# The second attention's first two adjacency tiles are prepared one phase earlier

## The reference, cut to what matters

```
qkv    = layernorm(x) @ Wqkv + bqkv
scores = q k^T / 8 + graph_bias * adj
scores = where(adj == 0, -1e9, scores)
x      = x + softmax(scores) v @ Wout + bout
```

## Time and profile before

| | |
|---|---|
| time, median of 3 runs | 2719.99 us (2716.86 to 2720.1) |
| the profiled execution: time | 2717.6 us |
| its span, and what lies around it | 2715.9 us, 1.7 us |
| p1: first DMA issued | 1144.85 us |
| a1: first DMA issued | 1224.11 us |
| first score added on DVE | 1239.55 us |

### The profile page before, as it was taken

One profiled execution on the slowest core, in us unless ns is written; L12 is line 12 of the kernel. 1 busy time (PEld: TensorE's weight loads), 2 busy tenths in 40 slices (PEclk: granted clock), 3 DMA queues, 4 the chain that ended last, 5 costly groups with the idle time before them and its releaser, 6 DMA issues. The chain is left out here.

```text
span 2715.9 us, 59651 instructions
## 1 busy us (share of the span) xinstructions
PE 2481.9 (91%) x20186; PEld 2029.7 (75%) x20187; DVE 2011.5 (74%) x4258; ACT 1614.1 (59%) x3050; POOL 1426.9 (53%) x1747
## 2 busy tenths in 40 slices
PE   6799999999975999097999999999689999999999
PEld 5377777777764998075777777777578888888888
DVE  5899989899945443787777777777667777777776
ACT  1577777777730332244666666666467777777775
POOL 6366666666451554432111122111388888888886
PEclk9799999999976999598999999999899999999999
DMA  2011111111054222301111111110000000000001
GB/s 99 21 43 49 56 43 43 43 63 43 22 197 148 70 72 62 126 16 35 55 41 41 41 41 41 45 58 21 7 1 0 0 0 0 0 0 0 0 0 41
DMA packets 43885, 114.26 MB, mean 42 GB/s; under 512 B 5621, under 2 KB 29918, under 8 KB 37982
## 3 DMA queue, kind: packets, MB, share of 16 engines
q1 hardware_dynamic: 38174, 97.16, 10.2%
q0 software_dynamic: 5568, 15.21, 1.8%
HBM read 99.21 MB, written 13.15 MB: 41 GB/s over the span
## 5 line engine op out<-in xcount | busy, mean ns | idle before, releaser
L2145 PE MATMUL f_pm<-f_wl,f_yt 128*128 128x256 f32 x2640 | 625.6, 380 | 0.0
L2145 PEld LDWEIGHTS f_pm<-f_wl,f_yt 128*128 128x128 f32 x2640 | 477.2, 191 | 51.6
L1089 POOL TENSOR_TENSOR ADJ<-ADJ,a_off 128x2708 f32<-128x2708 f32 x22 | 131.2, 5962 | 543.1 <-DVE ADJ L1168 543.1
L118 POOL TENSOR_SCALAR f_yy<-f_th,f_rs 128x255 f32<-128x255 f32 x660 | 367.5, 573 | 21.8 <-POOL f_rs L113 21.8
L526 ACT COPY a_wt<-a_tp 128x512 f32<-128x512 f32 x528 | 256.9, 566 | 155.3 <-PE a_tp L732 155.3
L1995 DVE SCALAR_TENSOR_TENSOR f_gg<-f_th,f_pm 128x512 f32<-128x512 f32 x319 | 219.0, 687 | 171.4 <-ACT f_th L2089 170.3
L549 POOL TENSOR_SCALAR a_off<-ADJ 128x677 bf16<-128x677 f32 x84 | 278.3, 3334 | 78.3 <-DMA ADJ<-in_adj 63.7
L626 DVE SCALAR_TENSOR_TENSOR a_lg<-a_f1s,F2S,a_fo 128x1024 f32<-128x1024 f32 (+1 forms) x264 | 294.5, 1152 | 30.8 <-issue 17.1
L1148 DVE CUSTOM_DVE_ANT_0 a_sc<-a_qk,ADJ 128x1024 f32<-128x1024 f32 (+1 forms) x264 | 288.3, 1093 | 30.4 <-PE a_qk L1246 30.4
L2089 ACT ACTIVATE f_th<-f_pm 128x512 f32<-128x512 f32 x319 | 190.5, 597 | 199.7 <-PE f_pm L2145 199.7
L1112 ACT ACTIVATE a_sc<-a_sc,a_mx 128x1024 f32<-128x1024 f32 (+1 forms) x264 | 277.7, 1052 | 45.3 <-DVE a_mx L1153 45.3
(11 more groups left out here) (295 smaller groups left out, 4572.0 us busy)
## 6 DMA issues: line engine op xcount, KB each, us to landing
ADJ<-in_adj SPq DMA_DIRECT2D x44, 1354.0 KB, 5.8
W<-in_L_ffn_w SPq DMA_DIRECT2D x32, 512.0 KB, 9.8
m_got<-YD SPq DMA_DIRECT2D x6, 768.0 KB, 10.4
out<-X SPq DMA_DIRECT2D x21, 128.0 KB
X<-in_x SPq DMA_DIRECT2D x3, 768.0 KB, 9.9
XD<-XF SPq DMA_DIRECT2D x3, 768.0 KB
m_b<-in_L_ffn_b SPq DMA_DIRECT2D x1, 2048.0 KB, 8.4
m_rows<-XD,SLOT POOLq DMA_INDIRECT x58, 2.8
```

The costliest lines, as they stand in the source:

```text
L118: return eng.tensor_scalar(out, x, rs[:, 0, bass.ds(t, 1)], rs[:, 1, bass.ds(t, 1)], ALU.mult, ALU.add)
L2145: mm = pe.matmul(out, yt[:, g, r, k, :], wl[:, k, :], start=(k == 0), stop=(k == KD - 1))
```

## The change

The three steps for the first two adjacency tiles move from the start of `a1` into `p1`; `off`, `gb` and their semaphores are allocated for both phases, and `gb` is loaded in `p1` ahead of the adjacency tiles. In `p1` DVE does `off` and the scaling of tile 0 after the statistics and before `results(0)`, and those of tile 1 after `results(4)`. POOL does the sum of tile 0 after it has normalised tile t = 5, and that of tile 1 after t = 15. In `a1` DVE goes straight to its first score. PE no longer waits ahead of its first score; it waits for `wout` alone, after the nine chunks, before its loop. POOL waits for `bout` alone.

```diff
+ADDED = (5, 15)
 def layer1_prepare(nc, io, keep, layer1):
...
             sp.dma_start(bv[:, :], bcast_rows(io["L1_gnn_bqkv"][2 * D:3 * D], P)).then_inc(b_in, 16)
-            first_adj(sp, io, layer1["ADJ1"], layer1["adj_in"])
+            sp.dma_start(gb[:, :], io["L1_gnn_graph_bias"].rearrange("a b c -> (a b) c").to_broadcast([P, 1])
+                         ).then_inc(gb_in, 16)
+            first_adj(sp, io, adj, adj_in)
...
                 standard_rows(pool, xn[:, t % 4:t % 4 + 1, :], X[:, t:t + 1, :], rs, t).then_inc(xn_done[b], 1)
+                if t in ADDED:
+                    k = ADDED.index(t)
+                    pool.wait_ge(scaled_adj[k], 1)
+                    pool.wait_ge(off_done[k], 1)
+                    pool.tensor_tensor(adj[:, k, :], adj[:, k, :], off[:, :], ALU.add).then_inc(bias_done[k], 1)
...
         def _(dve):
+            def first_tile(k):
+                dve.wait_ge(adj_in[k], 16)
+                if k:
+                    dve.wait_ge(bias_done[0], 1)
+                else:
+                    dve.wait_ge(gb_in, 16)
+                dve.tensor_scalar(off[:, :], adj[:, k, :], 0.0, MASKED, ALU.is_equal, ALU.mult).then_inc(off_done[k], 1)
+                dve.wait_ge(off_done[k], 1)
+                dve.tensor_scalar(adj[:, k, :], adj[:, k, :], gb[:, :], None, ALU.mult).then_inc(scaled_adj[k], 1)
             dve.memset(V[:, :, :, HD:VW], 1.0)
             slot_moments(dve, X, st, mom, stats, folded, moments)
             dve.wait_ge(b_in, 32)
+            first_tile(0)
...
             for i in range(NPAIR):
                 results(i)
+                if 2 * i + 1 == ADDED[0] + 4:
+                    first_tile(1)
...
 def layer1_attention(nc, io, keep, layer1):
...
-            sp.dma_start(gb[:, :], io["L1_gnn_graph_bias"].rearrange("a b c -> (a b) c").to_broadcast([P, 1])
-                         ).then_inc(gb_in, 16)
-            sp.dma_start(wout[:, :, :], io["L1_gnn_Wout"].rearrange("(k p) o -> p k o", p=P)).then_inc(w_in, 16)
-            sp.dma_start(bout[:, :], bcast_rows(io["L1_gnn_bout"], P)).then_inc(w_in, 16)
+            sp.dma_start(wout[:, :, :], io["L1_gnn_Wout"].rearrange("(k p) o -> p k o", p=P)).then_inc(wout_in, 16)
+            sp.dma_start(bout[:, :], bcast_rows(io["L1_gnn_bout"], P)).then_inc(bout_in, 16)
...
-            for b in range(2):
-                bias(0, b)
-            pool.wait_ge(w_in, 32)
+            pool.wait_ge(bout_in, 16)
...
-            dve.wait_ge(gb_in, 16)
-            for b in range(2):
-                off_tile(0, b)
-                scale_tile(0, b)
...
-            pe.wait_ge(w_in, 32)
             for h in range(3):
                 for c in range(NC):
                     scores((0, 0, h), c)
+            pe.wait_ge(wout_in, 16)
```

More of the change, by code:

```diff
@@ L797, in _ @@
             turn_back(last_unit(H - 2))
+ADDED = (5, 15)
 def layer1_prepare(nc, io, keep, layer1):
     X, V, ident, neg_half = (keep[n] for n in ("X", "V", "ident", "neg_half"))
-    QT, KH, KL = (layer1[n] for n in ("QT", "KH", "KL"))
+    QT, KH, KL, off, gb, adj, adj_in, off_done, scaled_adj, bias_done = (
+        layer1[n] for n in ("QT", "KH", "KL", "OFF1", "GB1", "ADJ1", "adj_in", "off_done", "scaled_adj", "bias_done"))
     W2 = 2 * P
@@ L822, in layer1_prepare @@
         pv = ph.ps("pv", [P, 2, 512])
-        (w_in, b_in, scaled, kept0, kept, stats, moments, inv, pchain, folded, masked,
+        (w_in, b_in, gb_in, scaled, kept0, kept, stats, moments, inv, pchain, folded, masked,
          turned, xt_done, qk_mm, full_done, high_done, low_done, placed, last_placed) = ph.sems(
-            "w_in b_in scaled kept0 kept stats moments inv pchain folded masked "
+            "w_in b_in gb_in scaled kept0 kept stats moments inv pchain folded masked "
             "turned xt_done qk_mm full_done high_done low_done placed last_placed")
@@ L1015, in layer1_attention @@
     X, V, ident = keep["X"], keep["V"], keep["ident"]
-    QT, KH, KL, adj, adj_in = (layer1[n] for n in ("QT", "KH", "KL", "ADJ1", "adj_in"))
+    QT, KH, KL, off, gb, adj, adj_in, off_done, scaled_adj, bias_done = (
+        layer1[n] for n in ("QT", "KH", "KL", "OFF1", "GB1", "ADJ1", "adj_in", "off_done", "scaled_adj", "bias_done"))
     with Phase(nc, "a1") as ph:
-        off = ph.sb("off", [P, N])
-        gb = ph.sb("gb", [P, 1])
         sc = ph.sb("sc", [P, H, N])
@@ L1033, in layer1_attention @@
         po = ph.ps("po", [P, 512])
-        off_done, scaled_adj, bias_done, qk_done, biased = (
-            ph.sems(f"{n}0 {n}1") for n in "off_done scaled_adj bias_done qk_done biased".split())
+        qk_done, biased = (ph.sems(f"{n}0 {n}1") for n in "qk_done biased".split())
         neg_max, exp_done = (ph.sems(" ".join(f"{n}{h}" for h in range(H))) for n in ("neg_max", "exp_done"))
@@ L1040, in layer1_attention @@
         turned, copied = (ph.sems(" ".join(f"{n}{k}" for k in range(TB))) for n in ("turned", "copied"))
-        summed, rec_done, spread_done, heads_in, heads_out, gb_in, w_in = ph.sems(
-            "summed rec_done spread_done heads_in heads_out gb_in w_in")
+        summed, rec_done, spread_done, heads_in, heads_out, wout_in, bout_in = ph.sems(
+            "summed rec_done spread_done heads_in heads_out wout_in bout_in")
         block = ph.block()
@@ L2214, in build @@
             layer1 = buffers(part, V1=([P, NT, H, VW],), QT=([P, H, NT * P], F16), KH=([P, H, N], F16),
-                             KL=([P, H, N], F16), ADJ1=([P, 2, N],))
+                             KL=([P, H, N], F16), ADJ1=([P, 2, N],), OFF1=([P, N],), GB1=([P, 1],))
+            for name in ("off_done", "scaled_adj", "bias_done"):
+                layer1[name] = [part.enter_context(nc.semaphore(f"{name}_of_tile{b}")) for b in range(2)]
             layer1["adj_in"] = adj_in[2:]
```

## The result

| | before | after |
|---|---|---|
| time, median of 20 runs each | 2718.16 us | 2722.18 us |
| profiled span | 2715.9 us | 2721.2 us |
| p1, from its first DMA to a1's first DMA | 79.26 us | 98.18 us |
| from a1's first DMA to its first transposes | 25.62 us | 11.69 us |

The ratio is 1.0014, with a 95% interval of 1.0007 to 1.0020: the changed kernel is slower by 1.9 to 5.4 us, 3.8 in the middle, which lies within the 0.2% that the prediction takes as no change, and is more than nothing. Of the 5.3 us between the two profiled spans 5.0 lie in the two stretches of the table: 18.9 paid in the preparation, 13.9 gained in the attention.

The account below looks back on a forecast made before the run. The prediction took PE, busy 91% of the span, as the bound; +8.5 (tile 0) + 6.9 (tile 1) - 13.6 (attention's start) = +1.8 us, so a median of 2721.8 us, range 2717 to 2728.

Parts of the forecast that it names:

- gain at the attention's start: Start of a1: with the chain of DVE and POOL gone, the transposes start about 13.6 us earlier (13.2 to 14.0).
- PE late through tile 0's sum: p1, pair 3: POOL's sum delays its tiles, so PE projects pair 2 7.4 us late (6.4 to 8.4).
- clock after it: p1, PE's restart at 1.2 GHz: 1.1 us after tile 0's stop; 0.5 after tile 1's, an even chance of 1.1.
- PE late through tile 1's sum: p1, pair 8: POOL's sum delays its tiles, so PE projects pair 7 6.4 us late (5.4 to 7.4).
- (a): The forecast itself: POOL's sums in p1 hold PE twice and pay back a1's gain, +1.8 us; chance 0.79.
- 6 to 8 that I named: Sign in p1: a gap of 6 to 8 us in PE's stream ahead of pair 3, released by POOL.
- 14 to 17 that I named: Sign at the end of p1: its last row comes 14 to 17 us later.
- Rival (b): p1: POOL's sums stay hidden and only DVE's delays remain, -11.5 us, 2708.5 us; chance 0.07.
- Rival (c): p1: DVE keeps POOL out through all of `place`, each sum 3.9 us later, +9.6 us, 2729.6 us; chance 0.09.
- alone moves nothing here: p1: DVE's small copies in `place` stand some 5 us until POOL's sum is over, without effect, since PE waits longer for POOL.
- Rival (d): Start of a1: something the chain hid, such as PE's or DVE's start after the barrier, holds it, +5.8 us; chance 0.05.
- the wait for `wout` costs nothing: a1, after the nine chunks: weights had let PE go at 1228.30, PE reaches the wait at about 1236; no cost.

Follow-up runs that it names:

- early_wait: Changed kernel with PE's waits for both output weights put back ahead of its first score; ratio to the kernel before 1.0026.
- tile0_moved: Changed kernel with only tile 0 moved; tile 1's mask and scaling stay in the attention, between the heads' scores; ratio to the kernel before 0.9991.
- dve_sums: Changed kernel with both tiles' sums done on DVE, scaling and sum in one instruction per half tile, none on POOL; ratio to the kernel before 0.9982.
- late_sums: Changed kernel with both POOL sums behind its last tile and DVE's passes over tile 1 after pair 7; ratio to the kernel before 0.9998.
- warm: Changed kernel with throw-away PE transposes, 38 ahead of pair 3's and 26 ahead of pair 8's; ratio to the kernel before 1.0004.

## Why the prediction was right, and where it was off

| step | forecast | measured in the profiles |
|---|---|---|
| gain at the attention's start | 13.6 (13.2 to 14.0) | 13.9 |
| PE late through tile 0's sum | 7.4 | 7.3 |
| clock after it | 1.1 | 2.3 |
| PE late through tile 1's sum | 6.4 | 6.7 |
| clock after it | 0.5 (even chance of 1.1) | 2.5 |
| sum | +1.8 (-1.1 to +4.8) | +5.0 in the profiles, +3.8 (1.9 to 5.4) in the ratio |

The measured values are starts of projections after the phase's first DMA. Pair 2: 28.70 us against 21.37. Pair 3: 36.61 against 26.99, so 9.62, of which 2.3 behind the stop. Pair 7: 65.79 against 49.46, 16.33, so 6.7 more. The rest of 18.9 is the second clock, 6.14 - 3.62. Both waits of the table hold a little of the slow clock too: from the first transposition behind the stop to the projection it took 0.96 and 1.08 us, where I had put 0.4.

The mechanism was the forecast one, (a). The gain is the chain of DVE and POOL at the attention's start; it is paid back because POOL's sum stands between two pairs that PE needs. Both waits came out within 0.3 us. That the sum would start behind low was read from one pair of tiles (2.13 us instead of 1.10), and it held. That it ended at 1169.77, where I had 1169.75, is chance: the phase began 0.53 us later in this trace, so that the sum ended 0.5 us early, and the slow transpositions took up the difference. The gap of 5.83 us ahead of pair 3 is below the 6 to 8 that I named, because the projection of pair 0 took 5.50 us instead of 4.70 and PE came later to the same wait; in early_wait it took 4.43 and the gap was 6.76. That both sums matter was shown by taking them apart: one alone costs 9.6 (tile0_moved), neither on POOL 9.0 (dve_sums), neither in the preparation 0.6 to 0.9. The order on POOL is the wait that ends last, not the only one of that size: with the order mended and the sums kept, 13.4 us are still paid (late_sums).

The term that was mis-sized is the clock: 1.6 forecast, 4.8 measured, and this is all of the difference between +1.8 and +5.0; by it the preparation ran 18.9 us over in place of the 14 to 17 that I named. I took 1.1 from one execution of the phase's first projection, 4.70 us, ahead of which PE had already worked for 2 us. The same projection, with the same 2 us ahead of it, cost 0.8 to 1.9 us over 3.62 in the twelve profiles, 1.9 in the changed kernel's own. Behind the stops, with 1 us of transpositions ahead, it started with the slow clock and kept it for 4.6 of 5.91 and 5.1 of 6.14 us. How much of the excess is the shorter work ahead and how much the draw isn't shown: in five projections behind a full stop (two each in the changed kernel and early_wait, one in tile0_moved) the price was 1.25 to 2.5 us, and early_wait, with the same preparation, had 4.87 and 5.61 us in the two places, 3.2 over in place of 4.8. For the second stop I gave even odds; it fell. That the clock's price is real, and not only a label on time that another engine would have taken, is shown for the second stop (3.62 instead of 6.14 in warm), and not for the first.

The time itself came nearer than the difference, 2721.8 forecast and 2722.18 measured, and that is luck: my base, the median of three runs, 2719.99, lay 1.8 us above the median of twenty, 2718.16. As a difference, the two profiles, +5.0, lie just above my -1.1 to +4.8, and the ratio of all executions, +3.8, inside.

Rival (b), sums that stay hidden, is out by the gaps of 5.83 and 4.23 us. Rival (c), DVE keeping POOL out through `place`, is out: the sums began right behind low. It was the other way round, POOL kept DVE out. I wrote that this "alone moves nothing here", which was right for the change and no more: in late_sums, where POOL is out of PE's way, it is what costs. The Trainium skill's rule ("SBUF — State Buffer", "Who interferes with whom") was thus the one to believe whole: in these traces the copy in 16 bits stands for the entire sum, 5.34, 5.33 and 5.88 us instead of 0.28. Rival (d), a hidden limit at the attention's start, is out: PE and DVE are ready with the first DMA. The step "the wait for `wout` costs nothing" held, and I had not said what early_wait shows: the same edit that is worth nothing alone is worth 3.2 us once the chain is gone.

What stays open: what the slow clock at pair 3 costs when it is taken away, since warm did not hold it there (1.7 us left), and how much of dve_sums' second cost is the lost lead and how much the place of the step.

## What to carry to other kernels

Work moved into an earlier phase is not free because the average load there is low; look for the step that the bounding engine needs next from the engine that takes the work, and for what that engine excludes while it works. Of the idle time in this preparation only one stretch could be used at its face value, the 2 us of DVE ahead of the first pair; 1.6 us of work put there and the rest reordered in the attention gave 9.8 us where the whole move lost 3.8. Where a stop of TensorE is in the forecast, price the restart by stretches that begin with the slow clock from their first matmul, in several executions, and give it as a range: here it was 1.25 to 2.5 us a stop.

## What the runs showed of the hardware

A DVE copy between 16-bit tiles and a GpSimd sum that reads SBUF did not run side by side: a copy issued behind the sum's start ended with it (5.34, 5.33 and 5.88 us instead of 0.28), and a sum let go 0.16 us behind the start of low lasted 6.81 to 6.84 us instead of 5.9. Pieces of 677 columns with a tile between them won nothing (1.50 and 1.71 us for such a copy). Beside the scores of the attention, which read PSUM and the adjacency tile, nobody stood: in the kernel before, the second sum and the scores (1240.69 and 1244.02, 1.22 and 1.23 us) took as long as alone.

```profile
1239.81 5.93 POOL L1089 TENSOR_TENSOR ADJ<-ADJ,a_off 128x2708 f32<-128x2708 f32 x1 [3.52 <-DVE ADJ L1168]
```

TensorE's clock (1.2 instead of 2.4 GHz) fell although the engine had done throw-away work until 2.3 us before the real one came, and held where the pause was 1.3 us. Behind five full stops it rose 3.5 to 6.2 us after the first transposition, by the mean clocks of single microseconds: the projection of pair 2, 3.62 us at the full clock, took 4.87, 5.66 and 5.91 us in three kernels that differ in nothing ahead of it.
